# Two-layer graph network on one core: x's scale, first masks and halves, and the aggregation, moved ahead of neighbour steps

## The chip, the cores and the metric

One core of a Trainium2 chip runs the whole program. The metric is device microseconds of one execution of the kernel, in which all inputs are read from HBM and the output is written back.

## What is computed

The inputs are `x` (4096 x 256), a sparse 0/1 matrix `adj` (4096 x 4096, int32, about 8 ones in a row), a second set of rows `neigh` (4096 x 256) and small weights. Cut to what matters:

```python
mask = (adj > 0); deg = sum(mask, axis=1)
agg = mask @ x / max(deg, 1)                                   # layer 0
out0 = relu(concat(x @ W_self + b_self, agg @ W_nb + b_nb) @ W_comb + b_comb)
x1 = layernorm(x + out0)

value = neigh @ Wv + bv                                        # layer 1
neib_att = tanh(neigh @ Wn1 + bn1) @ Wn2 + bn2
x_att = tanh(x1 @ Wx1 + bx1) @ Wx2 + bx2
ws = leaky_relu(x_att @ neib_att.T)
p = softmax(where(adj > 0, ws, -9e15), axis=1)
result = layernorm(x1 + concat(x1 @ Wfx + bfx, p @ value))
```

## The kernel before

Every float32 operand of a large product is split into two float16 halves, a high one and a low one (`x16`, `v16`, `n16`), so that TensorE can run at its float16 rate. The halves are scaled first: VectorE finds the largest absolute value of a tensor, GpSimd takes the maximum over the partitions, and VectorE makes a power of two from it. For `x` these steps are `scan_x` (L525), the reduce on L669, the all-reduce on L459 and `x_scale_chain` (L514). ScalarE then makes the high halves of four blocks of rows (`x_high(i)`, L860) and VectorE the low halves (`x_low(i)`, L543); eight such turns cover `x`.

The neighbours also come in eight turns of four blocks. One turn is, on TensorE, `rows_turn` (transposes, L1013), `neigh_products` (values and the hidden layer's input, L1024), `neigh_hidden` (L1037) and `neigh_attention` (L1042); on ScalarE `copy_rows_t`, `copy_h`, `v_high`, `hidden` and `n_high` (L834 to L858); on VectorE `v_low` (L536) and `n_low` (L530). Each hands over to the next through semaphores. There is one buffer for the attention product, so `neigh_attention(t)` waits for `n_low(t-1)`.

`adj` is read in 32 blocks of 128 rows, each in four quarters of 1024 columns. VectorE turns a quarter into a bfloat16 mask (`make_mask(b, q)`, L549), SyncE's queue sends it through a transposing DMA (`turn_mask`, L374) and loads the next block's quarter behind it. TensorE multiplies the transposed mask by the halves of `x` (`aggregate(b, k)`, L1114; k counts eight groups of four column blocks, 8 matmuls each). For block 0 group k needs `x_low(k)`; a quarter serves two groups. After group 7 come the mean (`degrees`, `mean_of`, `mean_transpose`, `mean_high`, `mean_low`), `combine`, `layer0`, the first layernorm and then layer 1.

All engines run in order. The first half of the neighbours' turns (0 to 3) stands ahead of the main loop, together with the products of the layer-0 weights. The main loop then runs over slots `s`, written out alike on every engine, eight slots to a block of rows. Each engine first does `first_part(s)`: with `PRE = 4` and `TURN_SLOTS = 3`, turn 4 + s // 3 of the neighbours is worked at slots 0 to 11 (products, `copy_h`, `v_high`, `v_low` at s % 3 = 0, `hidden` and the next `rows_turn` at 1, `neigh_attention`, `n_high`, `n_low` at 2), and VectorE does `x_low(s + 1)` there. VectorE has one-off work on the side: `scale_x_attention` at slot 1, `late_weight_bounds` at 3, `scale_late_weights` at 5, `m_low` at 6 and 7, `split_wx1` at 8 and 10, `split_fx` at 9. After `first_part`, `aggregate(0, k)` has slot k, `aggregate(1, k)` slot 8 + k; `degrees(0)` is at slot 8, `mean_low(0)` at 11, `combine(0)` at 12, `layer0(0)` at 13. `MASK_SLOTS` (-7, -5, -1, 0) places block 1's four quarters at slots 1, 3, 7 and 8.

Of the kernel before, what the change touches and what calls it, by code (L numbers as in the profile page):

```python
# [22 lines left out]
NQ = N // QW  # L23
# [25 lines left out]
NT = NB // TR  # L49
# [42 lines left out]
PRE = 4  # L92
# [4 lines left out]
def due(s, at, k=None):  # L97

    b, g = divmod(s - at, NG)
    return (b, g) if 0 <= b < NB and (k is None or g == k) else None  # L100


def turn_due(s, at):

    t, part = divmod(s, TURN_SLOTS)
    return PRE + t if part == at and 0 <= t < NT - PRE else None
# [13 lines left out]
def gnn_kernel(nc, x, adj, w_self, b_self, w_nb, b_nb, w_comb, b_comb, neigh, wx1, bx1, wx2, bx2,  # L120
# [5 lines left out]
    with ExitStack() as ctx:  # L126
# [76 lines left out]
        def joint(turn):  # L203
            both = agg_both if turn == 1 else s_both
            return both[:, :, :].rearrange("p k (u n) -> p (k u) n", u=2)[:, :, 0:VH]
# [296 lines left out]
        def _(dve):  # L502
            scale_count = [0]

            def scale_link(ins):
                ins.then_inc(scale_step, 1)
                scale_count[0] += 1
                dve.wait_ge(scale_step, scale_count[0])

            def power_below(dst, src):  # L510
                scale_link(dve.tensor_scalar(dst, src, TINY, None, ALU.max))
                scale_link(dve.tensor_scalar(dst.bitcast(U32), dst.bitcast(U32), 0x7F800000, None, ALU.bitwise_and))

            def x_scale_chain():  # L514
                power_below(x_pow, x_top)
                scale_link(dve.reciprocal(x_scale, x_pow))
                dve.tensor_scalar(x_scale, x_scale, TOP, None, ALU.mult).then_inc(x_scaled, 1)
                dve.wait_ge(x_scaled, 1)
# [11 lines left out]
            def n_low(turn):  # L530
                dve.wait_ge(natt_hi, turn + 1)
                part = n16[2 * H:H3, GW * turn:GW * (turn + 1)]
                dve.scalar_tensor_tensor(out=part, in0=ps_x[2 * H:H3, :], scalar=bn2_sb[2 * H:H3, 0:1], in1=part,
                                         op0=ALU.add, op1=ALU.subtract).then_inc(natt_lo, 1)

            def v_low(turn):  # L536
                part = slice(TR * turn, TR * (turn + 1))
                dve.wait_ge(v_hi_made, turn + 1)
                dve.scalar_tensor_tensor(out=v16[:, part, V_LO:VW], in0=joint(turn)[:, :, 0:DV], scalar=v_scale,
                                         in1=v16[:, part, 0:DV], op0=ALU.mult,  # L540
                                         op1=ALU.subtract).then_inc(v_lo_made, 1)

            def x_low(i):  # L543
                part = slice(TR * i, TR * (i + 1))
                dve.wait_ge(x_hi_made, i + 1)
                dve.scalar_tensor_tensor(out=x16[:, part, X_LO:X_LO + D], in0=x_sb[:, part, :], scalar=x_scale,  # L546
                                         in1=x16[:, part, X_HI:X_HI + D], op0=ALU.mult, op1=ALU.subtract).then_inc(x_lo_made, 1)

            def make_mask(b, q):  # L549
                dve.wait_ge(adj_in[q], 16 * (b + 1))  # L550
                at_least(dve, mask_t_in[q], 16 * (b - MASK_BUFS + 1))
                at_least(dve, score_made, NG * (b - MASK_BUFS) + 2 * q + 2)
                if b == 2 and q == 0:
                    dve.wait_ge(m_done, DC + 1)
                if b == 3 and q == 0:
                    dve.wait_ge(natt_done, NT)
                dve.tensor_scalar(mask[:, b % MASK_BUFS, q * QW:(q + 1) * QW], adj_sb[:, q, :], 0.0, EDGE,  # L557
                                  ALU.is_le, ALU.add).then_inc(mask_made, 1)
# [108 lines left out]
                scan_x(i)  # L667
            dve.wait_ge(x_scanned, NT)
            dve.tensor_reduce(x_top, tops[:, 1, :], AX.X, ALU.max).then_inc(x_top_made, 1)  # L669
            n_low(2)  # L670
            dve.wait_ge(x_top_reduced, 1)
            x_scale_chain()
            v_low(3)
            x_low(0)
            for q in range(NQ):
                make_mask(0, q)

            def first_part(s):
                if s + 1 < NT:
# [147 lines left out]
        def _(act):  # L827
# [17 lines left out]
            def v_high(turn):  # L845
                act.wait_ge(v_done, turn + 1)
                act.activation(v16[:, TR * turn:TR * (turn + 1), 0:DV], joint(turn)[:, :, 0:DV], ACT.Copy, scale=v_scale).then_inc(v_hi_made, 1)

            def hidden(turn):
                act.wait_ge(h_done, turn + 1)  # L850
                at_least(act, natt_done, turn)
                act.activation(h_t, ps_h[:, 0:P], ACT.Tanh, bias=bn1_sb[:, 0:1]).then_inc(h_tanh, 1)

            def n_high(turn):
                act.wait_ge(natt_done, turn + 1)
                act.wait_ge(bounds_scaled, 1)
                act.activation(n16[:, GW * turn:GW * (turn + 1)], ps_x[0:H3, :], ACT.Identity,
                               bias=bn2_sb[0:H3, 0:1]).then_inc(natt_hi, 1)  # L858

            def x_high(i):  # L860
                act.wait_ge(x_scaled, 1)
                part = slice(TR * i, TR * (i + 1))
                act.activation(x16[:, part, X_HI:X_HI + D], x_sb[:, part, :], ACT.Copy, scale=x_scale).then_inc(x_hi_made, 1)
# [24 lines left out]
            copy_rows_t(PRE)  # L888
            copy_h(3)
            v_high(3)  # L890
            hidden(3)
            n_high(2)
            x_high(0)
            x_high(1)

            def first_part(s):
                if s == 0:
                    n_high(PRE - 1)
                if (t := turn_due(s, 0)) is not None:
                    copy_h(t)  # L900
                    v_high(t)
                if (t := turn_due(s, 1)) is not None:
                    hidden(t)
                    if t + 1 < NT:
                        copy_rows_t(t + 1)
                if (t := turn_due(s, 2)) is not None:
                    n_high(t)
                if s + 2 < NT:
                    x_high(s + 2)
                if s in (6, 7):  # L910
                    act.wait_ge(m_scaled, 1)
                    act.activation(m16[:, 0, s - 6, :], m_both[:, s - 6, :], ACT.Copy, scale=m_scale).then_inc(m_hi_made, 1)
# [97 lines left out]
        def _(pe):  # L1010
# [31 lines left out]
            def neigh_attention(turn):  # L1042
                pe.wait_ge(h_tanh, turn + 1)
                at_least(pe, natt_lo, turn)
                if turn == 0:
                    pe.wait_ge(att_copied, TR)
                for u in range(TR):
                    mm = pe.matmul(ps_x[0:H3, u * P:(u + 1) * P], wn2_u[:, u, :], h_t, start=True, stop=True)
                mm.then_inc(natt_done, 1)
# [48 lines left out]
            neigh_hidden(3)  # L1098

            def first_part(s):  # L1100
                if s == 0:
                    neigh_attention(PRE - 1)
                if (t := turn_due(s, 0)) is not None:
                    neigh_products(t)
                if (t := turn_due(s, 1)) is not None:
                    neigh_hidden(t)
                    if t + 1 < NT:
                        rows_turn(t + 1)
                if (t := turn_due(s, 2)) is not None:
                    neigh_attention(t)  # L1110
                if s == Z_BIAS_SLOT:
                    combine_biases()
# [107 lines left out]
            def x_attention(b):  # L1220
                pe.wait_ge(tanh_split, b + 1)
                pe.matmul(ps_x[0:H3, 0:P], wx2_16[:, :], tanh16[:, :], start=True, stop=True).then_inc(xatt_done, 1)

            for s in range(0, SLOTS + 3):
                first_part(s)
                if d := turned_by_pe(s, TURN_AT):
                    turn_p(*d)
                if d := due(s, 0):
                    aggregate(*d)
                if d := due(s, MEAN_T_AT, 0):  # L1230
                    mean_transpose(d[0])
                if d := due(s, COMBINE_AT, 0):
                    combine(d[0])
                if d := due(s, X1_T_AT, 0):
                    x1_transpose(d[0])
                if d := due(s, HIDDEN_AT, 0):
                    hidden_and_fx(d[0])
                if d := due(s, XATT_AT, 0):
                    x_attention(d[0])
                if d := due(s, SCORE_AT):  # L1240
                    scores(*d)
                if d := turned_by_pe(s, WEIGH_AT):
                    weigh_values(*d[0:2])
                for w, at in enumerate(WIDE_WEIGH_AT):
                    if (d := due(s, at)) and d[1] < 2:
                        weigh_values(d[0], BY_PE + 2 * w + d[1])
# [23 lines left out]
```

## Time and profile before

| | us |
|---|---|
| median of 3 runs | 728.27 |
| lowest and highest run | 727.76, 729.59 |
| the profiled execution | 729.11 |
| its span, first to last instruction | 727.3 |
| VectorE, ScalarE, GpSimd busy in the span | 622.4, 571.3, 130.7 |

Busy time is summed over the instructions of an engine. A wait is idle time just ahead of an instruction, and the trace names the instruction or transfer whose end released it. Matmuls overlap, so the length given for a group of them is longer by about 0.16 us than the distance to the next one. Programs' names have their digits cut: `s_both<-mask,neigh_sb` L1033 is a neighbours' product, `ps_x<-mask` L1048 the attention product, `agg_both<-x,mask_t` L1129 and L1132 the aggregation, and on VectorE `v` L539, `n` L533, `x` L546 and `mask` L557 are `v_low`, `n_low`, `x_low` and `make_mask`.

### The profile page before, as it was taken

Reading aid. Unit: us, or ns where it says so; the run is one execution under the profiler, and the core shown is the slowest. Engines: PE = TensorE matmul, PEld = TensorE weight load, DVE = VectorE, ACT = ScalarE, POOL = GpSimd, SP = SyncE. Lnnn points to the kernel's source line nnn. Section 1 sums busy time; section 2 is a strip of 40 time slices with the busy share of each in tenths; the row PEclk is TensorE's granted clock in tenths of the full one; section 3 lists DMA queues with packets and bytes.
Section 4 is the critical chain, followed back from the end, with each engine's and each line's share of the span. In section 5 each row is a group of like instructions: output and inputs, shape, how many; then the busy total and the mean of one; then the engine's idle time right before and its main releaser. Section 6 shows DMA issues by size and latency. Waiting matters only on the chain.

```text
span 727.3 us, 19837 instructions
## 1 busy us (share of the span) xinstructions
PE 677.6 (93%) x7368; PEld 599.3 (82%) x7368; DVE 622.4 (86%) x1537; ACT 571.3 (79%) x928; POOL 130.7 (18%) x243
## 2 busy tenths in 40 slices
PE   5779889999999999999999999999999999997775
PEld 4668767888888888988888888888888888886554
DVE  5888578999989999999999999999999999987863
ACT  2555248888888888888888888888888888889893
POOL 0010121212222211222211112222111222212101
PEclk9999999999999999999999999999999999999997
DMA  8977999999999999999999999999999999731222
GB/s 258 370 168 163 251 286 239 195 213 213 195 220 197 194 226 204 200 219 211 221 219 203 212 223 194 215 218 191 219 206 205 210 206 214 165 75 37 38 37 44
DMA packets 260312, 141.40 MB, mean 194 GB/s; under 512 B 225528, under 2 KB 243832, under 8 KB 260216
## 3 DMA queue, kind: packets, MB, share of 16 engines
q1 hardware_dynamic: 259688, 140.10, 90.3%
q8 instruction: 59, 0.97, 0.6%
q14 instruction: 37, 0.30, 0.1%
q10 hardware_dynamic: 528, 0.03, 0.0%
HBM read 81.37 MB, written 4.19 MB: 118 GB/s over the span
## 4 chain that ended last, share of the span: by engine, by line
PE 78%; DVE 5%; ACT 5%; issue 4%; DMA 3%; SPq 3%; POOL 1%; POOLq 0%; ACTq 0%; DVEq 0%
PE ps_v L1174 21%; PE agg_both L1129 14%; PE agg_both L1132 14%; PE ps_t L1153 10%; PE s_both L1144 7%; PE agg_both L1193 3%; PE agg_both L1196 3%; DMA neigh_sb<-neigh_sb 2%; PE s_both L1033 1%; PE ps_x L1213 1%; PE ps_x L1216 1%; ACT score L936 1%; DMA neigh_sb<-in_L_gnn_neigh_dram 1%; SPq L405 1%; PE agg_both L1184 1%
## 5 line engine op out<-in xcount | busy, mean ns | idle before, releaser
L1129 PE MATMUL agg_both<-x,mask_t 128*128 128x257 f16 x1024 | 244.0, 274 | 3.1 <-DMA mask_t<-mask 3.1
L1132 PE MATMUL agg_both<-x,mask_t 128*128 128x256 f16 x1024 | 237.9, 274 | 1.6 <-DVE x L546 1.6
L930 ACT ACTIVATE score<-s_both,sc 128x512 f32<-128x512 f32 x256 | 178.4, 697 | 63.9 <-PE s_both L1144 58.2
L707 DVE CUSTOM_DVE_ANT_0 score<-score,mask 128x512 f32<-128x512 f32 x256 | 176.0, 687 | 16.8 <-ACT score L930 14.3
L1174 PEld LDWEIGHTS ps_v<-v,late 128*128 128x128 f16 x2304 | 144.0, 97 | 41.2 <-DVE late L771 16.6
L1174 PE MATMUL ps_v<-v,late 128*128 128x129 f16 (+1 forms) x2304 | 162.7, 219 | 11.3 <-DVE late L788 5.7
L936 ACT ACTIVATE score<-score,exp_bias,sc 128x1024 f32<-128x1024 f32 x128 | 159.2, 1244 | 3.2 <-DVE exp_bias L716 3.2
L771 DVE TENSOR_TENSOR late<-ps_t,late 128x512 f16<-128x512 f32 x192 | 130.8, 681 | 33.1 <-ACT late L943 31.3
L943 ACT CAST late<-ps_t 128x512 f16<-128x512 f32 x192 | 114.4, 596 | 20.5 <-PE ps_t L1153 20.5
L1153 PE MATMUL ps_t<-ident,score 128*128 128x128 f32 x768 | 116.8, 275 | 4.0 <-ACT score L936 3.7
L1129 PEld LDWEIGHTS agg_both<-x,mask_t 128*128 128x128 fp8e4 x1024 | 100.6, 98 | 17.3 <-DMA mask_t<-mask 3.3
L1132 PEld LDWEIGHTS agg_both<-x,mask_t 128*128 128x128 fp8e4 x1024 | 100.4, 98 | 12.3 <-issue 1.7
L1144 PE MATMUL s_both<-n,stack 96*128 96x512 f16 x256 | 97.3, 380 | 1.0 <-DVE stack L761 0.9
L557 DVE TENSOR_SCALAR mask<-adj_sb 128x1024 bf16<-128x1024 int32 x128 | 89.8, 704 | 4.0 <-issue 0.2
L1153 PEld LDWEIGHTS ps_t<-ident,score 128*128 128x128 f32 x768 | 80.9, 141 | 5.8 <-ACT score L936 5.6
L487 POOL TENSOR_SCALAR mv<-mv 128x1 f32<-128x1 f32 x32 | 18.9, 592 | 234.9 <-DVE mv L794 234.9
L1174 PEld LDWEIGHTS ps_v<-v,neigh_sb 128*128 128x128 f16 x768 | 49.3, 98 | 11.5 <-DMA neigh_sb<-neigh_sb 4.1
L1174 PE MATMUL ps_v<-v,neigh_sb 128*128 128x129 f16 (+1 forms) x768 | 54.9, 221 | 2.6 <-DMA neigh_sb<-neigh_sb 2.6
L473 POOL TENSOR_SCALAR mv<-mv 128x1 f32<-128x1 f32 x32 | 7.8, 244 | 246.1 <-DVE mv L745 246.1
L776 DVE TENSOR_TENSOR neigh_sb<-score,neigh_sb 128x1024 f16<-128x1024 f32 x32 | 39.2, 1225 | 1.0
L482 POOL TENSOR_TENSOR late<-x,bfv_sb 128x256 f32<-128x256 f32 x32 | 27.8, 868 | 45.2 <-ACT x L954 45.2
L948 ACT CAST neigh_sb<-score 128x1024 f16<-128x1024 f32 x32 | 34.7, 1085 | 0.0
(140 smaller groups left out, 801.0 us busy)
## 6 DMA issues: line engine op xcount, KB each, us to landing
adj_sb<-in_adj_dram SPq DMA_DIRECT2D x128, 512.0 KB, 5.3
neigh_sb<-in_L_gnn_neigh_dram SPq DMA_DIRECT2D x8, 512.0 KB, 7.9
score<-in_x_dram SPq DMA_DIRECT2D x8, 512.0 KB, 8.6
x_in<-in_x_dram SPq DMA_DIRECT2D x32, 128.0 KB, 3.0
out_dram<-out_sb SPq DMA_DIRECT2D x32, 128.0 KB, 3.5
mask_t<-mask SPq DMA_TRANSPOSE x128, 4.7
neigh_sb<-neigh_sb SPq DMA_TRANSPOSE x64, 4.0
mask<-in_L_gnn_W_comb_dram SPq DMA_DIRECT2D x1, 512.0 KB, 8.0
```

The source lines that it names most:

```text
L557: dve.tensor_scalar(mask[:, b % MASK_BUFS, q * QW:(q + 1) * QW], adj_sb[:, q, :], 0.0, EDGE, ALU.is_le, ALU.add).then_inc(mask_made, 1)
L707: dve.tensor_tensor_reduce(score[:, b % 2, part], score[:, b % 2, part], mask[:, b % MASK_BUFS, part], 1.0, -3.0e38, ALU.subtract, ALU.max ...
L771: dve.tensor_tensor(p_lo[:, n % 2, :], ps_t[n % 2][:, :], p_hi[:, n % 2, :], ALU.subtract).then_inc(p_lo_made, 1)
L776: dve.tensor_tensor(wide_p[:, w, 1, :], score[:, b % 2, w * QW:(w + 1) * QW], wide_p[:, w, 0, :], ALU.subtract).then_inc(wide_lo_made[w], 1)
L930: act.activation(score[:, b % 2, k * GW:(k + 1) * GW], ps_s[k % 2][:, :], ACT.Prelu, alpha=SLOPE, scale=score_scale).then_inc(leaky_made, 1)
L936: act.activation(part, part, ACT.Exp, bias=exp_bias[:, b % 2:b % 2 + 1], scale=score_unit).then_inc(exp_made, 1)
L943: act.copy(p_hi[:, n % 2, :], ps_t[n % 2][:, :]).then_inc(p_hi_made, 1)
L1129: mm = pe.matmul(agg[:, 0:D + 1], mask_t8[:, c, 0, :], x16[:, c, X_HI:X_ONE + 1], start=(c == 0), stop=(c == NC - 1), skip_group_check=True)
L1132: mm = pe.matmul(agg[:, 0:D], mask_t8[:, c, 0, :], x16[:, c, X_LO:X_LO + D], start=False, stop=False, skip_group_check=True)
L1144: pe.matmul(ps_s[k % 2][:, :], stack[:, b % 2, :], n16[:, k * GW:(k + 1) * GW], start=True, stop=True).then_inc(s_done, 1)
L1153: mm = pe.transpose(ps_t[n % 2][:, u * P:(u + 1) * P], score[:, b % 2, at:at + P], ident[:, :])
L1174: mm = pe.matmul(ps_v[:, 0:n], p, v16[:, c, v:v + n], start=(j == 0 and u == 0 and part == 0), stop=(j == NG - 1 and u == CG - 1 and part ...
```

## The change

Four orders are changed; no instruction is added, taken away or altered.

- VectorE, ahead of the loop: the scale of x is computed as soon as the all-reduce returns, and then come `make_mask(0, 0)` and `x_low(0)`; `n_low(2)`, the other three quarters and `v_low(3)` follow. Before, `n_low(2)` stood ahead of the scale and `v_low(3)` and `x_low(0)` ahead of all masks.
- ScalarE, ahead of the loop: `x_high(0)` goes ahead of `hidden(3)` and `n_high(2)`.
- ScalarE, in `first_part(s)`: `x_high(s + 2)` goes ahead of the neighbours' steps of the slot.
- TensorE, in the loop: `neigh_attention(3)` stays ahead of everything, but in every slot `aggregate` goes ahead of `first_part(s)`, that is ahead of the products, transposes and attention product of the slot (and of `combine_biases` at slot 2).

```diff
@@ VectorE, ahead of its loop
             dve.tensor_reduce(x_top, tops[:, 1, :], AX.X, ALU.max).then_inc(x_top_made, 1)
-            n_low(2)
             dve.wait_ge(x_top_reduced, 1)
             x_scale_chain()
+            make_mask(0, 0)
+            x_low(0)
+            n_low(2)
+            make_mask(0, 1)
             v_low(3)
-            x_low(0)
-            for q in range(NQ):
-                make_mask(0, q)
+            make_mask(0, 2)
+            make_mask(0, 3)
@@ ScalarE
             v_high(3)
+            x_high(0)
             hidden(3)
             n_high(2)
-            x_high(0)
             x_high(1)
 
             def first_part(s):
                 if s == 0:
                     n_high(PRE - 1)
+                if s + 2 < NT:
+                    x_high(s + 2)
                 if (t := turn_due(s, 0)) is not None:
                     copy_h(t)
                     v_high(t)
...
                     n_high(t)
-                if s + 2 < NT:
-                    x_high(s + 2)
@@ TensorE
             def first_part(s):
-                if s == 0:
-                    neigh_attention(PRE - 1)
...
+            neigh_attention(PRE - 1)
             for s in range(0, SLOTS + 3):
-                first_part(s)
                 if d := turned_by_pe(s, TURN_AT):
                     turn_p(*d)
                 if d := due(s, 0):
                     aggregate(*d)
+                first_part(s)
```

## Rows read from the trace of the kernel before

**Rows 1.** The profile page's first part: busy time and share of the span by engine.

```profile
PE 677.6 (93%) x7368; PEld 599.3 (82%) x7368; DVE 622.4 (86%) x1537; ACT 571.3 (79%) x928; POOL 130.7 (18%) x243
```

**Rows 2.** Stretches: length, busy us and (instructions) by engine, TensorE clock, DMA share, GB/s.

```profile
38.00:48.00 10.00, 4.62 (x34) 3.96 (x33) 7.39 (x13) 6.44 (x10) 2.73 (x4) 0.97 0.41 82
...
200.00:300.00 100.00, 99.92 (x1134) 89.05 (x1132) 90.83 (x231) 84.92 (x138) 19.48 (x35) 1.00 1.03 212
```

**Rows 3.** Timeline of PE: start us, us, line, operation, count, [idle before <- releaser].

```profile
40.87 1.09 PE L1048 MATMUL ps_x<-mask 128*96 128x128 f32 x8 [1.90 <-DVE n L533]
...
47.84 0.40 PE L1129 MATMUL agg_both<-x,mask_t 128*128 128x257 f16 x1 [3.07 <-DMA mask_t<-mask]
```

**Rows 4.** Timeline of VectorE from the top of x to the first masks, same columns.

```profile
37.61 0.16 DVE L669 TENSOR_REDUCE sc<-tops 128x1 f32<-128x8 f32 x1
39.97 0.75 DVE L533 SCALAR_TENSOR_TENSOR n<-ps_x,bn_sb,n 32x512 f16<-32x512 f32 x1 [2.20 <-ACT n L857]
...
41.51 0.75 DVE L539 SCALAR_TENSOR_TENSOR v<-s_both,sc,v 128x512 f16<-128x512 f32 x1
42.70 1.28 DVE L546 SCALAR_TENSOR_TENSOR x<-score,sc,x 128x1024 f16<-128x1024 f32 x1 [0.43 <-ACT x L863]
43.90 2.49 DVE L557 TENSOR_SCALAR mask<-adj_sb 128x1024 bf16<-128x1024 int32 x4
```

**Rows 5.** Timeline of GpSimd, the all-reduce of the top of x.

```profile
37.87 0.37 POOL L459 PARTITION_ALL_REDUCE sc<-sc  x1 [15.05 <-DVE sc L669]
```

**Rows 6.** Timeline of ScalarE, the third `n_high` and the first two `x_high`.

```profile
39.00 0.37 ACT L852 ACTIVATE mask<-ps_v,bn_sb 128x128 f32<-128x128 f32 x1
39.27 0.67 ACT L857 ACTIVATE n<-ps_x,bn_sb 96x512 f16<-96x512 f32 x1
41.51 2.19 ACT L863 ACTIVATE x<-score,sc 128x1024 f16<-128x1024 f32 x2 [1.57 <-DVE sc L517]
```

**Rows 7.** Timeline of SyncE's queue, the issue of the first mask transpose.

```profile
44.61 1.35 SPq L377 DMA_TRANSPOSE mask_t<-mask  x1
```

**Rows 8.** Timeline of VectorE through the setup's neighbour steps.

```profile
48.43 0.75 DVE L539 SCALAR_TENSOR_TENSOR v<-s_both,sc,v 128x512 f16<-128x512 f32 x1
...
55.80 1.27 DVE L546 SCALAR_TENSOR_TENSOR x<-score,sc,x 128x1024 f16<-128x1024 f32 x1
58.76 0.75 DVE L539 SCALAR_TENSOR_TENSOR v<-s_both,sc,v 128x512 f16<-128x512 f32 x1 [1.68 <-ACT v L847]
...
61.60 2.48 DVE L546 SCALAR_TENSOR_TENSOR x<-score,sc,x 128x1024 f16<-128x1024 f32 x2
64.11 0.75 DVE L533 SCALAR_TENSOR_TENSOR n<-ps_x,bn_sb,n 32x512 f16<-32x512 f32 x1
...
66.17 1.28 DVE L546 SCALAR_TENSOR_TENSOR x<-score,sc,x 128x1024 f16<-128x1024 f32 x1
...
69.64 0.75 DVE L624 SCALAR_TENSOR_TENSOR m<-late,sc,m 128x512 f16<-128x512 f32 x1 [0.74 <-ACT m L912]
...
74.21 0.75 DVE L539 SCALAR_TENSOR_TENSOR v<-s_both,sc,v 128x512 f16<-128x512 f32 x1 [0.70 <-ACT v L847]
...
77.73 0.48 DVE L729 SCALAR_TENSOR_TENSOR mean_t<-agg_both,sc,mean_t 128x256 f16<-128x256 f32 x1
```

**Rows 9.** Timeline of PE through the same stretch.

```profile
55.50 2.33 PE L1033 MATMUL s_both<-mask,neigh_sb 128*128 128x160 f32 x16
...
63.03 0.27 PE L1132 MATMUL agg_both<-x,mask_t 128*128 128x256 f16 x1 [1.56 <-DVE x L546]
...
67.10 1.03 PE L1020 MATMUL ps_t<-ident,neigh_sb 128*128 128x128 f32 x8
...
78.36 0.81 PE L1193 MATMUL agg_both<-m,x_t 128*128 128x256 f16 x6 [0.63 <-DVE mean_t L729]
```

**Rows 10.** One-us stretches around the end of PE's longest wait; clock is third from last.

```profile
46.00:47.00 1.00, 0.00 (x0) 0.00 (x0) 1.00 (x2) 0.70 (x1) 1.00 (x2) 1.00 1.13 210
...
48.00:49.00 1.00, 1.00 (x6) 0.70 (x5) 0.97 (x2) 0.00 (x0) 0.56 (x2) 0.50 0.78 284
```

## The prediction

> **What bounds the kernel now.** I read the page's busy times first: TensorE (PE) leads with 93% of the span, but VectorE has 86% [rows 1]. A share of the whole hides the stages, so next the table of stretches. From 200 to 300 us PE is busy 99.92 of 100 us: in the steady part PE alone sets the pace, and work comes out of it as late or as early as it went in. From 38 to 48 us, where this change acts, PE is busy 4.6 of 10 us and VectorE 7.4 [rows 2]. So a microsecond won or lost before the steady part should reach the end whole, and the question is which engine's queue leads there.
>
> The timelines answer it. PE's longest wait in the stretch is 3.07 us at 47.84 for the first transposed mask, after 1.90 us at 40.87 for `n_low(2)` [rows 3]. The mask is late because VectorE made it at 43.90, behind a 2.20 us wait for `n_high(2)` and 0.43 us for `x_high(0)` [rows 4]. After 47.84 it is still VectorE that leads: `aggregate(0, 5)` waits 1.56 us for `x_low(5)`, and `combine(0)` 0.63 us for `mean_low(0)` [rows 9], which follows the last neighbour step in VectorE's queue. VectorE waits only 1.68, 0.74 and 0.70 us more up to 77.73 [rows 8]; with the first two that is 5.75 us of waits from 37.77 to `mean_low(0)`. Everything else there is work whose amount the change keeps. So the sum can be made on VectorE: its new waits against these 5.75 us.
>
> **The early part.** The top of x is ready at 37.77; GpSimd's all-reduce runs from 37.87 for 0.37 us [rows 4, 5]. The scale chain can start at 38.35. Its four small steps took 0.78 us (from the end of `n_low(2)` at 40.72 to 41.51, [rows 4]); it ends at 39.1. How soon after GpSimd's span VectorE really goes on isn't shown, since it was held by ScalarE till 39.97; so the bounds are 38.35 and 39.97 and I take the near one, because GpSimd's span is the nearest row.
>
> `make_mask(0, 0)` then takes 0.62 (four took 2.49, [rows 4]), to 39.75. `x_high(0)` starts at 39.1, and `x_low` followed it by 1.19 (41.51 to 42.70, [rows 4, 6]): VectorE waits 0.55 us, `x_low(0)` starts at 40.3 and ends at 41.6. ScalarE does `hidden(3)` and `n_high(2)` behind `x_high(0)`: 40.2, 40.5 to 41.15 instead of 39.0 to 39.94 [rows 6], 1.2 us later but hidden behind `x_low(0)`. `n_low(2)` starts at 41.65, `make_mask(0, 1)` at 42.35, `v_low(3)` at 42.95, the other two masks at 43.6 and 44.2, `x_low(1)` at 44.85. Before, `x_low(1)` came right behind the masks, at 46.3. So VectorE is 1.45 us ahead here, having waited 1.15 us where it waited 2.63. The first mask is 4.8 us earlier; its transpose took 3.23 us from issue to PE's start [rows 3, 7] and so lands at 43.1. SyncE's queue has nothing else then; the transposes and the loads of `adj` behind them come some 4 us early and wait for nobody.
>
> **PE's new order.** `neigh_attention(3)` needs `n_low(2)`, now at 42.4 instead of 40.7. PE was done with its last step at 38.97 [rows 3], so it now waits 3.5 us in one piece. Then 0.9 us of attention product, 0.9 us of `aggregate(0, 0)` (0.11 us a matmul: 63.03 to 67.10 holds two groups, one product turn of 2.2 and little else [rows 9]), and only then the products of turn 4. At full clock these start at 44.4; before they lay in the dead time ahead of 47.84 for nothing. From a product turn's start to `v_low`'s start took 3.26 us (55.50 to 58.76, [rows 8, 9]). So `v_low(4)` starts at 47.7, and VectorE, ready at 47.0, waits 0.7 us. It is now 0.7 us ahead of before (48.43).
>
> From there each aggregation stands ahead of the neighbour work of its slot, and inherits the wait for `x_low`:
> - From the start of `v_low(4)` to the end of `x_low(4)` took 8.64 us [rows 8]: the latter ends at 56.3. `aggregate(0, 3)` follows `x_low(3)` and the biases, starting at 53.6, so the products of turn 5 start at 54.5 (before 55.50) and `v_low(5)` at 57.8. VectorE waits 1.5 us (before 1.68).
> - `x_low(5)` comes 2.84 us behind `v_low(5)` (58.76 to 61.60, [rows 8]): 60.65, and PE, 1.43 us behind it (61.60 to 63.03), starts `aggregate(0, 5)` at 62.05. Before, `neigh_attention(5)` had been done in PE's gap, ahead of this wait. Now it starts at 62.95; with 1.07 to `n_high` and 0.7 to `n_low`, `n_low(5)` starts at 64.7, while VectorE is free at 63.15 (60.65 + 2.5). That is a wait of 1.5 us that wasn't there, and puts VectorE 0.6 us behind before (64.11).
> - `x_low(7)` starts 2.06 behind it (64.11 to 66.17), 66.75; `aggregate(0, 7)` at 68.15. Only then `neigh_hidden(6)` and `rows_turn(7)`, at 69.15 instead of 67.10 [rows 9]. ScalarE copies these ahead of its `m16(1)`, for which `m_low(1)` waits; that came 2.54 us behind `rows_turn(7)`'s start (67.10 to 69.64, [rows 8, 9]). Now 71.65: VectorE waits 2.2 instead of 0.74 and is 2.0 us behind.
> - `v_low(7)` waits 0.7 as before. `n_low(7)` has its attention product behind `aggregate(1, 2)` and `aggregate(1, 3)`: another 0.5. `mean_low(0)` at about 80.1 instead of 77.73, `combine(0)` at 80.8 instead of 78.36.
>
> VectorE's waits add up to 0.6 + 0.55 + 0.7 + 1.5 + 1.5 + 2.2 + 0.7 + 0.5 = 8.25 us against 5.75: the order alone costs 2.4 us (2.5 by the waits). PE's own gaps say the same: it is early by up to 4 us and then waits for `x_low` ahead of groups 2, 5 and 7. From `combine(0)` on the order is as before, the first block's chain of small steps follows, and the shift stays.
>
> **The clock.** In the trace TensorE still has 1.00 at 46 to 47, in the middle of the 3.07 us wait, and 0.50 (1.2 of 2.4 GHz) at 48 to 49, right behind it [rows 10]; after the 1.90 us wait the attention product took 1.09 us for 8 matmuls, its full-clock length [rows 3]. Now PE waits 3.5 us ahead of `neigh_attention(3)` and, with group 4, `neigh_hidden(5)` and `rows_turn(6)` done by 58.6, 3.4 us ahead of `aggregate(0, 5)`. Both are longer than the wait that brought the level down, so I expect it down after the first. Attention product and first aggregation then take 1.75 us each instead of 0.9; 1.5 us of that reaches `v_low(4)` and all that follows. Before, the low level struck when VectorE's queue led anyway and cost little. After the second gap `aggregate(0, 5)` and `neigh_attention(5)` are both ahead of `n_low(5)`: 1.75 us at most, nothing at least (the level may fall later or not at all). I take the middle, 0.9.
>
> The Trainium skill, page "TensorE: Matmul & The Clock Gate", Part 1, has the low level as the default, which "activity releases"; this case's trace agrees, with 0.50 behind the long wait. By that rule alone both gaps would cost in full, and the sum would be 5.7 us instead of 4.8.
>
> **The sum.** 2.4 + 1.5 + 0.9 = +4.8 us. On the profiled execution (729.11 us, of which 727.3 is span) that is 733.9; it lies 0.84 above the median 728.27, so the predicted time is 733.1 us.
>
> **Rivals.**
> - Order alone, clock kept at full in both gaps: 728.27 + 2.4 = 730.7. For it: the level outlasted most of the 3.07 us wait. Chance 0.20, split between slower and no change.
> - Losses absorbed: VectorE's new waits are there, but the small steps' distances shrink when the queues are less full, and the waits at `m_low(1)` and `n_low(7)` (1.45 and 0.5 more) go. Then some 0.5 us stays, 728.8; the range of this case is 727.5 to 730. Against it: the distances that I used are from moments when the receiving engine was waiting. Chance 0.16.
> - Faster, the other side: VectorE's start decides. It is 1.45 us ahead at `x_low(1)`, and if `v_low(4)` starts by 47.0 it keeps that; if the products of turn 5, a microsecond early, then also cover the 1.68 us wait at `v_low(5)` by 1.1, `mean_low(0)` comes 2.5 us early and the time is 725.7. It decides at `v_low(4)`: before 47.0 the product turn must have started before 43.8, which needs the aggregation ahead of it to be done by then; the mask lands at 43.1 at best. Chance 0.10, a third of it within 0.3%.
> - Worse: both gaps cost in full and the all-reduce holds VectorE up to 1.6 us longer than its span says; 735.5 and above. That is also the case in which the change doesn't do what it says, as the scale is hardly earlier. Chance 0.06.
>
> **How the numbers follow.** The forecast case (732 to 735.4) has 0.48. The range 728.6 to 735.4 leaves out the faster case, the worst and the low end of the absorbed one. About 0.3% (2.2 us) is what a measurement of this kernel can tell from no change. Slower by more: 0.48 + 0.12 + 0.06 = 0.66. Within: 0.08 + 0.16 + 0.03 = 0.27. Faster: 0.07.
>
> **What would show it.** In the changed kernel's trace, measured from the top of x: the first mask some 4.8 us earlier; a 3.5 us PE wait ahead of `neigh_attention(3)`, with matmuls of 0.22 us behind it; VectorE waiting at `v_low(4)`, at `n_low(5)` (before none) and over 2 us at `m_low(1)`; `combine(0)` beyond 80 us. The prediction falls if `v_low(4)` starts before 47 us, if `n_low(5)` doesn't wait, or if `combine(0)` is late but the steady part isn't.

## The result and the profile after

| | before | changed |
|---|---|---|
| median of 6 runs, us | 729.42 | 734.92 |
| lowest, highest, us | 727.76, 730.16 | 734.17, 737.37 |
| profiled execution and its span, us | 729.11, 727.3 | 737.37, 735.6 |

The changed kernel takes 1.0090 times as long (95% interval 1.0074 to 1.0105), about 6.6 us more; the two medians in the table differ by 5.5. In a second comparison (below) the ratio was 1.0062 (1.0039 to 1.0086), about 4.5 us. The forecast was +4.8 us, 733.1 us. Two executions of one kernel below, the kernel before with its wait filled, took 888.52 and 2481.2 us; its median counts them, its ratio leaves them out, and their cause isn't known.

The page's first line shows the same work in a longer span; beside [rows 1], VectorE's sum is unchanged, and PE's is 5.4 us larger although it has the same matmuls:

```profile
PE 683.0 (93%) x7368; PEld 604.5 (82%) x7368; DVE 622.4 (85%) x1537; ACT 571.7 (78%) x928; POOL 129.7 (18%) x243
```

VectorE's timeline of the changed kernel, to be read against [rows 4, 8]. Columns are start, length, line, operation, and in brackets the wait before it and its releaser:

```profile
40.22 0.16 DVE L669 TENSOR_REDUCE sc<-tops 128x1 f32<-128x8 f32 x1
40.87 0.15 DVE L511 TENSOR_SCALAR sc<-sc 128x1 f32<-128x1 f32 x1 [0.49 <-POOL sc L459]
...
43.02 1.28 DVE L546 SCALAR_TENSOR_TENSOR x<-score,sc,x 128x1024 f16<-128x1024 f32 x1 [0.69 <-ACT x L865]
...
53.11 0.75 DVE L539 SCALAR_TENSOR_TENSOR v<-s_both,sc,v 128x512 f16<-128x512 f32 x1 [3.34 <-ACT v L849]
...
63.29 0.75 DVE L539 SCALAR_TENSOR_TENSOR v<-s_both,sc,v 128x512 f16<-128x512 f32 x1 [1.87 <-ACT v L849]
...
71.45 0.75 DVE L533 SCALAR_TENSOR_TENSOR n<-ps_x,bn_sb,n 32x512 f16<-32x512 f32 x1 [2.84 <-ACT n L859]
...
75.12 0.75 DVE L539 SCALAR_TENSOR_TENSOR v<-s_both,sc,v 128x512 f16<-128x512 f32 x1 [0.33 <-ACT v L849]
...
78.36 0.75 DVE L624 SCALAR_TENSOR_TENSOR m<-late,sc,m 128x512 f16<-128x512 f32 x1 [1.82 <-ACT m L914]
...
82.92 0.75 DVE L539 SCALAR_TENSOR_TENSOR v<-s_both,sc,v 128x512 f16<-128x512 f32 x1 [0.69 <-ACT v L849]
...
86.16 0.75 DVE L533 SCALAR_TENSOR_TENSOR n<-ps_x,bn_sb,n 32x512 f16<-32x512 f32 x1 [0.53 <-ACT n L859]
...
90.52 0.18 DVE L747 BATCH_NORM_AGGREGATE mv<-stat 128x2 f32<-128x6 f32 x1
```

The top of x (L669) comes 2.6 us later than in the trace of before, though nothing ahead of it differs in order; this is a difference between executions (where it arises is said further down), so distances below are counted from this instruction. The last row is the last step of `layer0(0)`. From the start of L669 to the start of this step it is 50.30 us. VectorE's timeline of before has this row for the same step:

```profile
81.31 0.18 DVE L745 BATCH_NORM_AGGREGATE mv<-stat 128x2 f32<-128x6 f32 x1
```

That is 43.70 us after its L669 at 37.61, so the stretch grew by 6.60 us. Its waits tell where: 3.34 us at `v_low(4)`, 2.84 at `n_low(5)` (none before), 1.82 at `m_low(1)` (0.74 before). Now PE in the same stretch, against [rows 3, 9]:

```profile
45.23 2.00 PE L1050 MATMUL ps_x<-mask 128*96 128x128 f32 x8 [3.19 <-DVE n L533]
...
48.73 3.46 PE L1035 MATMUL s_both<-mask,neigh_sb 128*128 128x160 f32 x16
...
67.56 0.27 PE L1132 MATMUL agg_both<-x,mask_t 128*128 128x256 f16 x1 [3.32 <-DVE x L546]
...
68.78 1.91 PE L1050 MATMUL ps_x<-mask 128*96 128x128 f32 x8
...
87.57 0.82 PE L1193 MATMUL agg_both<-m,x_t 128*128 128x256 f16 x6 [1.27 <-DVE mean_t L731]
```

Two waits of over 3 us, ahead of `neigh_attention(3)` (L1050) and of `aggregate(0, 5)` (L1132), and behind each an attention product of 1.9 to 2.0 us where 8 such matmuls took 1.09 us in [rows 3]. The granted clock is the third number from the end:

```profile
43.00:44.00 1.00, 0.00 (x0) 0.00 (x0) 0.98 (x1) 1.00 (x3) 0.00 (x0) 1.00 0.34 66
...
45.00:46.00 1.00, 0.77 (x4) 0.80 (x5) 0.94 (x3) 0.00 (x0) 0.00 (x0) 0.50 0.89 175
...
50.00:51.00 1.00, 1.00 (x6) 1.00 (x5) 0.00 (x0) 0.00 (x0) 0.29 (x1) 0.50 1.35 306
51.00:52.00 1.00, 1.00 (x9) 0.99 (x8) 0.00 (x0) 0.00 (x0) 0.00 (x0) 1.00 1.09 255
...
67.00:68.00 1.00, 0.44 (x4) 0.42 (x5) 1.00 (x2) 0.00 (x0) 0.00 (x0) 1.00 0.60 113
...
69.00:70.00 1.00, 1.00 (x6) 1.00 (x6) 0.00 (x0) 0.00 (x0) 0.00 (x0) 0.50 0.62 197
```

It is still at 1.00 at 43 to 44, inside the first wait, falls before that wait has ended (0.59 on average over 44 to 45), and is at 0.50 (1.2 of 2.4 GHz) until 51 us, over the attention product, the first aggregation and part of the products of turn 4. The second time it falls behind the wait, during `aggregate(0, 5)` (0.53 over 68 to 69), and is at 0.50 until 71.

Behind the stretch nothing more is lost. VectorE's first step of `layer1` (L784) in the timeline of before:

```profile
133.75 0.16 DVE L784 RECIPROCAL row<-ps_v 128x1 f32<-128x1 f32 x1
```

The same step in the changed kernel:

```profile
142.96 0.16 DVE L786 RECIPROCAL row<-ps_v 128x1 f32<-128x1 f32 x1
```

In both traces that is 52.44 us behind the last step of `layer0(0)`. From one block's L784 to the next it is then 19.50 us in both (a single one 19.74), with PE busy throughout as in [rows 2], until the blocks near the end, which take less. A shift made in the setup is neither recovered nor added to before the last blocks.

### The profile page after: what moved, and what is told of

Its sections match the earlier page's. It is cut to its first block, busy times and chain, and to the rows that moved or that the text cites. A ratio compares the mean times of both kernels' runs of the same rounds, so it can differ in the third digit from the quotient of the medians.

```text
span 735.6 us, 19837 instructions
## 1 busy us (share of the span) xinstructions
PE 683.0 (93%) x7368; PEld 604.5 (82%) x7368; DVE 622.4 (85%) x1537; ACT 571.7 (78%) x928; POOL 129.7 (18%) x243
## 4 chain that ended last, share of the span: by engine, by line
PE 83%; DVE 6%; ACT 5%; issue 3%; DMA 2%; POOL 1%; SPq 0%; POOLq 0%; ACTq 0%
PE ps_v L1174 22%; PE agg_both L1129 14%; PE agg_both L1132 14%; PE ps_t L1153 11%; PE s_both L1144 7%; PE agg_both L1193 3%; PE agg_both L1196 3%; PE s_both L1035 2%; PE ps_x L1213 1%; PE ps_x L1216 1%; DMA neigh_sb<-in_L_gnn_neigh_dram 1%; ACT score L938 1%; PE agg_both L1184 1%; PE ps_x L1050 1%; PE ps_x L1207 1%
## 5 line engine op out<-in xcount | busy, mean ns | idle before, releaser
L1132 PE MATMUL agg_both<-x,mask_t 128*128 128x256 f16 x1024 | 238.8, 274 | 5.5 <-DVE x L546 5.5
L1132 PEld LDWEIGHTS agg_both<-x,mask_t 128*128 128x128 fp8e4 x1024 | 100.6, 98 | 17.2 <-issue 6.5
```

What stands on the lines that cost most here:

```text
L1132: mm = pe.matmul(agg[:, 0:D], mask_t8[:, c, 0, :], x16[:, c, X_LO:X_LO + D], start=False, stop=False, skip_group_check=True)
```

## Experiments

All differ from the kernel before or the changed kernel only as the diffs say. "The stretch" is the time from the start of L669 to the start of `layer0(0)`'s last step, 43.70 us in the trace of before and 50.30 in that of the changed kernel. In the first comparison (first four kernels) the kernel before had a median of 729.79 us, in the second (next four) 730.06, in the third (last two) 729.24.

**One engine's part alone.** The changed TensorE order, the rest as before:

```diff
             def first_part(s):
-                if s == 0:
-                    neigh_attention(PRE - 1)
...
+            neigh_attention(PRE - 1)
             for s in range(0, SLOTS + 3):
-                first_part(s)
...
                     aggregate(*d)
+                first_part(s)
```

> Only the change on TensorE: aggregate ahead of first_part in every slot, VectorE and ScalarE in the order of before. Theory (PE's new order makes the neighbour steps inherit the waits for masks and x_low, and VectorE then waits for them): the first mask lands as late as before, so the products of turn 4 wait for it, v_low(4) starts some 15.7 us after the top of x (before 10.8, changed kernel 12.9), and the time is 8 to 10 us above before. Rival (the early scale, masks and x halves on VectorE and ScalarE cause the loss, for instance n_low(2) being late): within 1.5 us of before.

Measured: 739.0 us, ratio 1.0132 (1.0096 to 1.0168), 9.2 us above before, as expected. In PE's timeline, the wait for the first mask:

```profile
47.71 0.40 PE L1127 MATMUL agg_both<-x,mask_t 128*128 128x257 f16 x1 [5.34 <-DMA mask_t<-mask]
```

In VectorE's, the top of x and `v_low(4)`:

```profile
36.87 0.16 DVE L669 TENSOR_REDUCE sc<-tops 128x1 f32<-128x8 f32 x1
...
53.64 0.75 DVE L539 SCALAR_TENSOR_TENSOR v<-s_both,sc,v 128x512 f16<-128x512 f32 x1 [5.12 <-ACT v L847]
```

`v_low(4)` starts 16.8 us after the top of x, 1.1 later than expected, and the stretch is 54.98 us. The granted clock was 0.50 from 42 to 51 us here, so this kernel's loss is that of the order and of a low clock together. The loss comes from TensorE's order, and the earlier mask only softens it. The other half, VectorE's and ScalarE's new order with TensorE as before:

> Only the changes on VectorE and ScalarE; TensorE does first_part ahead of aggregate as before. Theory: VectorE is 1.5 us ahead at x_low(1) and PE's neighbour steps wait for no aggregation, so the time is 1 to 2.5 us below before (ratio 0.997 to 0.999), with VectorE's waits at v_low(4) and n_low(5) near zero. Rival (the early scale costs): 2 to 6 us above before.

Measured: 727.16 us, ratio 0.9964 (0.9947 to 0.9982), 2.6 us below before, just beyond the 1 to 2.5 expected. The stretch is 40.59 us, 3.1 shorter. VectorE's timeline, the top of x, `v_low(4)` and `v_low(5)`:

```profile
37.97 0.16 DVE L669 TENSOR_REDUCE sc<-tops 128x1 f32<-128x8 f32 x1
...
47.58 0.75 DVE L539 SCALAR_TENSOR_TENSOR v<-s_both,sc,v 128x512 f16<-128x512 f32 x1 [0.26 <-ACT v L849]
...
56.01 0.75 DVE L539 SCALAR_TENSOR_TENSOR v<-s_both,sc,v 128x512 f16<-128x512 f32 x1
```

PE's timeline, `neigh_attention(3)`:

```profile
42.78 1.08 PE L1050 MATMUL ps_x<-mask 128*96 128x128 f32 x8 [3.23 <-DVE n L533]
```

`v_low(4)` waits 0.26 us, and `v_low(5)` at 56.01 not at all (1.68 before). So the early scale is a gain by itself, and both halves together lose it again. PE's wait of 3.23 us is there too, yet this trace shows full clock behind it (8 matmuls in 1.08 us).

**The clock.** Unread matmuls in the two long waits of the changed kernel:

```diff
+            def keep_busy(n):
+                for _ in range(n):
+                    pe.matmul(ps_agg[1][:, 0:P], ident[:, :], ident[:, :], start=True, stop=True)
+            pe.wait_ge(m_copied, DC)
+            keep_busy(16)
             neigh_attention(PRE - 1)
...
+                if s == 5:
+                    pe.wait_ge(z_bias_made, 1)
+                    keep_busy(16)
                 if d := due(s, 0):
```

> The changed kernel plus 2 x 16 matmuls whose result nobody reads (identity by identity, into a PSUM bank that is free then), in PE's two long waits: ahead of neigh_attention(3) and ahead of aggregate(0, 5). Each set takes 1.8 us of a wait of over 3 us. Theory (the low clock behind these two waits is on the path): the granted clock stays at 1.00 through both, the matmuls behind them take 0.11 us, v_low(4)'s wait falls from 3.3 to about 1 us and n_low(5)'s from 2.8 to 1.5, and the time is 3.5 to 4.5 us below the changed kernel, 2 to 3 us above before. Rival (PE's clock doesn't matter while VectorE leads, only the order does): same as the changed kernel, 5.5 to 6.5 us above before.

Measured: 729.72 us, ratio 1.000 (0.9982 to 1.0018). The clock is 1.00 throughout the stretch, and VectorE's timeline has these waits at `v_low(4)`, `v_low(5)`, `n_low(5)` and `m_low(1)`:

```profile
47.66 0.75 DVE L539 SCALAR_TENSOR_TENSOR v<-s_both,sc,v 128x512 f16<-128x512 f32 x1 [0.54 <-ACT v L849]
...
57.85 0.75 DVE L539 SCALAR_TENSOR_TENSOR v<-s_both,sc,v 128x512 f16<-128x512 f32 x1 [1.87 <-ACT v L849]
...
64.89 0.75 DVE L533 SCALAR_TENSOR_TENSOR n<-ps_x,bn_sb,n 32x512 f16<-32x512 f32 x1 [1.72 <-ACT n L859]
...
71.80 0.75 DVE L624 SCALAR_TENSOR_TENSOR m<-late,sc,m 128x512 f16<-128x512 f32 x1 [2.12 <-ACT m L914]
```

A set of 16 such matmuls, two records each in the trace, takes 3.74 us on PE and not the 1.8 of the expectation, so it fills the whole wait. It hardly delays what follows: from L669 to `aggregate(0, 5)` it is 24.43 us here and 24.35 in the second trace of the changed kernel (below). The stretch is 46.19 us: 4.1 shorter than in the changed kernel's trace, and 2.5 longer than in the trace of before. The waits came as expected. The time didn't: it was to be 2 to 3 us above before and is level with it. The control below has one reason for that.

The attention product put back ahead of the aggregation:

```diff
             def first_part(s):
...
-                if (t := turn_due(s, 2)) is not None:
-                    neigh_attention(t)
...
             for s in range(0, SLOTS + 3):
+                if (t := turn_due(s, 2)) is not None:
+                    neigh_attention(t)
...
                     aggregate(*d)
                 first_part(s)
```

> The changed kernel with one step put back: neigh_attention(t) of slots 2, 5, 8 and 11 goes ahead of the slot's aggregate, the products and transposes stay behind it. Theory: n_low(5) no longer waits behind x_low(5) (2.8 us in the changed kernel), and PE's wait ahead of aggregate(0, 5) is shorter by 0.9 us and less likely to bring the clock down; the time is 3 to 4 us below the changed kernel, 2 to 3 us above before. Rival (the loss is in the first gap and the products of turn 4 alone): within 1 us of the changed kernel.

Measured: 731.43 us, ratio 1.0032 (1.0011 to 1.0053), as expected; that is 2.2 to 4.2 us below the changed kernel by its three ratios. The stretch is 47.27 us, 3.0 shorter than in the changed kernel's first trace. PE's wait ahead of `aggregate(0, 5)` is 1.84 us and the clock stays at 1.00 behind it, so the 3.0 us are those of the step put back and of the second fall together. `n_low(5)` at 66.72 has no wait; `v_low(4)` still has all of its own (VectorE's timeline):

```profile
51.18 0.75 DVE L539 SCALAR_TENSOR_TENSOR v<-s_both,sc,v 128x512 f16<-128x512 f32 x1 [3.34 <-ACT v L849]
...
61.37 0.75 DVE L539 SCALAR_TENSOR_TENSOR v<-s_both,sc,v 128x512 f16<-128x512 f32 x1 [1.87 <-ACT v L849]
...
66.72 0.75 DVE L533 SCALAR_TENSOR_TENSOR n<-ps_x,bn_sb,n 32x512 f16<-32x512 f32 x1
```

**Does it repeat?** The changed kernel once more:

> The changed kernel once more, beside the others on one chip, for the size of the loss and to see whether both low-clock stretches are there in a second trace. Theory: 5 to 7 us above before; layer0(0) starts 48 to 49 us after the top of x again (before 42.3; with the filled gaps 44.7), v_low(4) waits over 3 us. Rival (the low clock behind the two waits was chance): layer0(0) at 46 to 47 us in this trace, 3 to 4 us above before.

Measured: 734.67 us, ratio 1.0062 (1.0039 to 1.0086), 4.6 us above before. The stretch is 47.45 us in this trace, and PE's timeline shows why it isn't 50, with `neigh_attention(3)` and `aggregate(0, 5)`:

```profile
42.46 1.08 PE L1050 MATMUL ps_x<-mask 128*96 128x128 f32 x8 [3.31 <-DVE n L533]
...
62.00 0.37 PE L1132 MATMUL agg_both<-x,mask_t 128*128 128x256 f16 x1 [3.32 <-DVE x L546]
```

VectorE's, with `v_low(4)` and `n_low(5)`:

```profile
47.54 0.75 DVE L539 SCALAR_TENSOR_TENSOR v<-s_both,sc,v 128x512 f16<-128x512 f32 x1 [0.54 <-ACT v L849]
...
66.03 0.75 DVE L533 SCALAR_TENSOR_TENSOR n<-ps_x,bn_sb,n 32x512 f16<-32x512 f32 x1 [2.98 <-ACT n L859]
```

The same 3.3 us wait ahead of `neigh_attention(3)` stands here with full clock behind it (8 matmuls in 1.08 us), and `v_low(4)` waits 0.54 instead of 3.34 us; only behind the second wait is the clock low. The rival was right for this one trace; the time, 4.6 us above before, lies between its 3 to 4 and the theory's 5 to 7. The traced run is one of the three fastest of nine (732.92 us; the other six took 734.5 to 736.2), so the first fall may be the commoner case; those runs have no traces that could show it. And the kernel before:

> The kernel before once more, one look, to see what in its trace repeats. Theory: from the top of x to layer0(0) 42.3 us give or take 1, the 53.9 us from there to the first layer1 the same within 0.1, and the differences between executions lie ahead of the top of x and in the last 20 us, where the clock is low or not. Rival: the stretch from the top of x to layer0(0) itself varies by 2 us or more.

Measured: 729.43 us. The stretch is 44.43 us, and 52.43 from there to the first layer 1. The attention product behind the 1.90 us wait took 1.76 us here, against 1.09 in [rows 3] (PE's timeline):

```profile
41.75 1.76 PE L1048 MATMUL ps_x<-mask 128*96 128x128 f32 x8 [1.90 <-DVE n L533]
```

So the same wait of the same kernel is followed by either level. `n_low(2)` waits 2.68 us here and 2.20 in [rows 4], with the low clock ahead of the top of x lasting until 31.8 us against 30.3: 0.48 us of this stretch's 44.43 come from there and not from the waits named here. The kernel before, with its wait ahead of the first aggregation filled:

```diff
                 first_part(s)
+                if s == 0:
+                    pe.wait_ge(m_copied, DC)
+                    keep_busy(16, ps_agg[1])
```

> The kernel before plus 16 matmuls whose result nobody reads, in PE's 3.07 us wait ahead of aggregate(0, 0). Theory (the low clock costs the kernel before too, which the prediction set at little): clock stays at 1.00 from 47 to 51 us, aggregate(0, 0) and rows_turn(5) run in 0.11 us steps, the products of turn 5 start 1.2 us earlier, v_low(5)'s wait falls from 1.7 to about 0.5, and the time is 1 to 1.5 us below before. Rival (VectorE leads there and the low clock is free): the same as before within 0.5 us.

Measured: 725.91 us, ratio 0.9955 (0.9935 to 0.9974), 3.3 us below before by the ratio, more than expected. The set of matmuls is longer than the wait of 3.07 us (PE's timeline), and `aggregate(0, 0)` starts 10.57 us after L669 instead of 10.23, yet the kernel gains:

```profile
44.22 3.73 PE L1226 MATMUL agg_both<-ident 128*128 128x128 f32 x32
```

The stretch is 42.64 us, 1.1 less than in the trace of before, and `v_low(5)` waits 1.00 instead of 1.68 (VectorE's timeline):

```profile
57.31 0.75 DVE L539 SCALAR_TENSOR_TENSOR v<-s_both,sc,v 128x512 f16<-128x512 f32 x1 [1.00 <-ACT v L847]
```

The version that the experiments point to, VectorE's and ScalarE's part with both long waits of its order filled (shown against that kernel; the bank is now a parameter of `keep_busy`):

```diff
             rows_turn(3)
+            pe.wait_ge(h_tanh, 2)
+            keep_busy(24, ps_v)
             neigh_products(2)
...
                 if s == 0:
+                    pe.wait_ge(m_copied, DC)
+                    keep_busy(16, ps_agg[1])
                     neigh_attention(PRE - 1)
```

> Only the changes on VectorE and ScalarE (TensorE's order of before), plus unread matmuls in PE's two waits of this order: 24 ahead of neigh_products(2) (wait of 4.3 us) and 16 ahead of neigh_attention(3) (3.2 us). Theory (both waits can bring the clock down, the first delays v_low(2) and so the scans of x): the top of x is ready 0.5 to 1 us earlier, no low clock from 22 us to the tail, and the time is 0.5 to 2 us below the same kernel unfilled, 3 to 4.5 us below before. Rival (this order leaves PE enough slack): same as unfilled, 2.6 us below before.

Measured: 723.66 us, ratio 0.9926 (0.9898 to 0.9955), 5.4 us below before by the ratio, more than expected: the fastest of all, ahead of both kernels. The granted clock is 1.00 in every stretch of its first 600 us; the other traces all have low clock somewhere between 24 and 34 us. Its stretch, 40.58 us, equals that of the unfilled kernel (40.59), whose trace was at full clock too. The top of x comes at 37.52 against 37.97 us; that the filling ahead of `neigh_products(2)` does this can't be told from the differences between executions (36.87 to 40.22 us where nothing ahead of it was filled), so that part of the expectation stays open. By the ratios the filling gains 2.8 us on the unfilled kernel, of which 1.0 us is in the last block of these traces (next paragraph). The trace of the unfilled kernel is that of its fastest run (725.14 us), so it can't show where the rest lies, and there is no control for this kernel.

**A control on the filling.** The last block, from the last L784 but one to the last (or the same instruction under its number in the other kernels), took 10.78 us in all three filled kernels and 11.75 to 12.98 in the seven others, far from where anything was filled. So 16 such matmuls in the kernel before and 32 in the changed one, at the very start (the diff is the first; the changed kernel has 32 in place of 16):

```diff
+            keep_busy(16, ps_v)
             rows_turn(0)
             rows_turn(1)
```

> Control for the filled kernels: the kernel before plus 16 unread matmuls at the very start of TensorE's program, where PE waits 8 us for the first neighbours' rows anyway and no later wait is shortened. In all three filled kernels the last block took 10.8 us, in all seven traces without filling 11.8 to 13.0. Theory (what filling the 3 us wait saves is the clock behind it; the last block is something else): same as before in the stretch from the top of x to layer0(0) (43.7 to 44.4 us to its last step); the time is the same as before within 0.3%. Rival (more matmuls in the program, wherever they stand, shorten the end): last block 10.8 us, and 1.5 to 2 us below before.

> The same control for the changed kernel: 32 unread matmuls, as many as in the filled changed kernel, but at the start of TensorE's program. Theory (the filled kernel's 5 us below the changed one is mostly the clock in the two waits): 3.5 to 6 us above before, at least one of the two low-clock stretches in the trace. Rival (it was the number of matmuls): as the filled kernel, within 1 us of before.

Measured: the kernel before with 16 of them 727.4 us, ratio 0.9978 (0.9956 to 0.9999), its stretch 43.16 us; the changed kernel with 32 of them 734.76 us, ratio 1.0083 (1.0058 to 1.0108), its stretch 49.28 us. The last block took 10.77 us in both. PE's last group in the timeline of before:

```profile
719.26 2.37 PE L1174 MATMUL ps_v<-v,neigh_sb 128*128 128x129 f16 x24 [1.06 <-DMA neigh_sb<-neigh_sb]
```

And with 16 matmuls at the start:

```profile
717.85 1.53 PE L1179 MATMUL ps_v<-v,neigh_sb 128*128 128x129 f16 x24
```

The transfer for which PE waited 1.06 us is there in time, and the clock is full. It is the transfer that goes with the added matmuls: a wait of 0.79 to 1.23 us for it is in all seven unfilled traces and in none of the five with added matmuls, while only two of the seven have the low clock behind it (these last blocks took 12.84 and 12.98 us, the others 11.75 to 12.02). So the rival holds for the end: in all five kernels with added matmuls, wherever they stand, the last block is 1 to 2 us shorter. The measured gain of filling is partly this. Against their controls the filled kernels gain 0.9955 / 0.9978, 0.2% or 1.7 us, in the kernel before, and 1.000 / 1.0083, 0.8% or 6 us, in the changed one. The intervals of these ratios are some 0.2% wide to each side, so the 0.2% isn't clear of noise and the 0.8% is. For the changed kernel the theory stands: its control kept the whole loss and both low-clock stretches. But the 6 us are an upper bound: the control's 32 matmuls ran until 11.9 us and so put off the first transposes, which started at 8.7 us in the filled kernel, and the top of x was ready at 38.74 us in it against 37.77. Whether the one caused the other wasn't tried; the stretches alone differ by 3.1 us (49.28 and 46.19). That the control of the kernel before is itself 1.6 us faster is in size what the shorter end gives.

## Why the prediction was right or wrong

Right were the sign, the engine, and the places. What failed are two sizes: the clock's term, put at 2.4 us (4.1 in the profiled execution, 2.8 in the mean of three), and the low clock's cost in the kernel before, put at nothing (1.1 in the mean of three). VectorE's waits, as forecast and as the traces have them (us):

| ahead of | forecast, full clock | forecast, low clock adds | filled | changed, again | changed |
|---|---|---|---|---|---|
| scale chain, `x_low(0)` | 0.6, 0.55 | | 0.50, 0.49 | 0.50, 0.49 | 0.49, 0.69 |
| `v_low(4)` | 0.7 | 1.5 | 0.54 | 0.54 | 3.34 |
| `v_low(5)` | 1.5 | | 1.87 | 1.87 | 1.87 |
| `n_low(5)` | 1.5 | 0.9 | 1.72 | 2.98 | 2.84 |
| `v_low(6)` | 0 | | 0 | 0 | 0.33 |
| `m_low(1)` | 2.2 | | 2.12 | 2.12 | 1.82 |
| `v_low(7)`, `n_low(7)` | 0.7, 0.5 | | 0.69, 0.52 | 0.70, 0.52 | 0.69, 0.53 |
| sum | 8.25 | 2.4 | 8.45 | 9.72 | 12.60 |

The changed kernel's 12.60 us against the 5.75 of before makes 6.85; the stretch grew by 6.60, since the trace of before has one more wait of 0.24 us that the rows don't show.

- **The early part** held: `make_mask(0, 0)`, `x_low(0)` and `n_low(2)` follow the top of x as written; the all-reduce gave a wait of 0.50 us and not the 1.6 more that the worst case allowed.
- **The order** was priced at 2.4 us against the trace of before; the filled kernel's stretch, at full clock throughout, is 2.49 us longer. Each new wait is within 0.4 us of its forecast. That the neighbour steps inherit the waits for masks and `x_low` is shown three ways: TensorE's order alone loses (+9.2 us, its low clock included), without it the rest gains (-2.6 us), and putting the attention product back removes the wait at `n_low(5)` and 2.2 to 4.2 us (the second fall included).
- **The clock** is the term that was mis-sized, twice. First in size: where it falls it costs 2.8 us at `v_low(4)` (3.34 against 0.54) and not 1.5, because it also lasts over the products of turn 4 (3.46 us against 2.34 at full clock), which I had at full clock; in the control, where it fell only behind the attention product, it costs 1.8 (2.38 against 0.54); and 1.1 to 1.3 us at `n_low(5)`, where I took 0.9. Both were down in the profiled execution: 4.1 us against 2.4. Second in kind: I took the first fall as certain, since 3.5 us is longer than the 3.07 us behind which it had come. It isn't: the same wait had the low clock behind it in the changed kernel's first trace and not in its second, and in the kernel before 1.90 us had it in one trace and not in another. Over the three traces of the changed order with its waits unfilled (the control among them) the stretch was 50.30, 47.45 and 49.28 us, a mean of 49.0 or 2.8 above the filled one.
- **The base** was wrong in a step that I had called small: "before, the low level struck when VectorE's queue led anyway and cost little". The filled kernel before has a stretch of 42.64 us, the unfilled ones 43.70, 44.43 and 43.16: 0.5 to 1.8 us. Not all of that is the clock behind the waits named: `n_low(2)` waits 2.20, 2.68 and 3.03 us in the three, because PE is later against the top of x where low clock ahead of it lasted longer; the changed order has no such wait. At full clock on both sides the order costs 46.19 - 42.64 = 3.55 us, and the low clock, wherever it lies, adds a mean of 2.8 to the changed kernel and 1.1 to the one before. Together 5.25 us, the difference of the means of three traces each (49.0 and 43.8); the measured ratios say 4.5 to 6.6. That the forecast of 4.8 came near them is in part luck: the order's own cost was put 1.15 us too low (2.4 for 3.55), and the low clock's, with the kernel before deducted, 0.7 too high (2.4 for 1.7).
- **The rule that was cited.** The Trainium skill, page "TensorE: Matmul & The Clock Gate", Part 1, also says that the moment at which the level rises differs between runs of the same kernel. For the fall the traces show the like: it came behind the first wait in one trace of the changed kernel and not in another (stretches of 50.30 and 47.45 us), and this, not the sentence that I cited, bore on the chance. By the cited rule alone the sum was 5.7 us; the measured 4.5 and 6.6 lie on both sides of it and of 4.8.
- **The shift stays** held: 52.4 us from the stretch's end to the first layer 1 in all traces but one (51.9), then 19.50 us a block but for a few of up to 19.92.
- **Not foreseen** was how far executions differ outside the stretch. In the changed kernel's profiled one the top of x is 2.6 us late, so that 737.37 us lies beyond the upper end of 735.4 while the median of 734.92 lies inside. Of this, 2.1 us are there by the top of the neighbours (L655 at 24.28 us against 22.19), after a wait of 2.62 us for a transfer of the neighbours' rows that took 0.24 in the trace of before; 0.5 more is `v_low(2)`'s wait (1.60 against 1.08 us) behind low clock. The rival "faster" needed `v_low(4)` 9.4 us after the top of x; even at full clock it came at 9.9 (37.65 to 47.54). "Losses absorbed" fell: the waits at `m_low(1)` and `n_low(7)` are there, and the 52.44 us behind the stretch are the same.

## What to carry to other kernels

When a step is put ahead of others in an in-order queue, everything behind it inherits its wait: list what the other engines expect from that queue during the wait. Here two orders that each looked like a gain on their own engine were a gain on one and a loss on the other, so try the halves apart. Where TensorE gets a wait of some 3 us in one piece, price the work behind it at both levels of the clock, and treat which of them comes as chance. Unread matmuls in the wait kept the clock at 1.00 in all three kernels in which it was tried; run a control with the same matmuls elsewhere beside them, and see that there it delays nothing.

## What was unexpected of the hardware

- The length of a wait didn't decide the clock behind it. The attention product's 8 matmuls took 1.08 to 1.76 us behind the wait of 1.90 us (five traces), 1.08 us behind waits of 3.23 and 3.31, and 1.99 and 2.00 us behind two waits of 3.19 us. In the control of the changed kernel they took 1.08 us behind 3.46 us, and the clock fell only after them: `v_low(4)` waited 2.38 us.
- The program's last block took 10.77 to 10.78 us in all five kernels with 16 to 40 unread matmuls, and 11.75 to 12.98 us in the other seven traces of five kernels, also when these matmuls ran 700 us earlier. What goes in all five is PE's wait for its last transposed tile (0.79 to 1.23 us); the low clock behind it (24 matmuls in 2.37 against 1.53 us) was there in two of the seven only. What joins it to the added matmuls wasn't found.
- The 12 runs of the filled changed kernel lay within 1.6 us (728.98 to 730.61), the 29 of the kernel before beside them over 6.8 us (726.18 to 732.96). The low clock's places may account for some of that; it wasn't measured.
